# Local attention layers: scores from 64-row halves, the cosine product of q moved from VectorE to GpSimd, and the loop over four units written out

## The reference

```python
def l2norm(t):
    return t / jnp.maximum(jnp.linalg.norm(t, axis=-1, keepdims=True), 1e-12)
...
def attn_layer(x, Wqkv, qs, ksc, Wo):
    b, n, _ = x.shape
    qkv = x @ Wqkv
...
    q = l2norm(q) * qs
    k = l2norm(k) * ksc
...
    q = q * cos * scale + rotate_half(q) * sin * scale
    k = k * cos * inv + rotate_half(k) * sin * inv
    out = local_attention(q, k, v)
    out = out.transpose(0, 2, 1, 3).reshape(b, n, INNER)
    return out @ Wo
...
for i in range(DEPTH):
    x = attn_layer(shift_tokens(x), Wqkv[i], q_scale[i], k_scale[i], Wo[i]) + x
    x = ffn_layer(shift_tokens(x), ln_g[i], ln_b[i], W1[i], b1[i], W2[i], b2[i]) + x
```

## Time and profile before

| | |
|---|---|
| runs, device time | 4602.41 us median of 3 (4593.22 to 4614.95) |
| profiled execution | 4612.28 us, its span 4610.5 us |
| granted TensorE clock, mean | 0.955 |
| busy: PE / PEld / DVE / ACT / POOL | 4030.1 / 3106.3 / 3777.2 / 2589.8 / 2029.8 us |
| instructions | 117054 |
| DMA | 138.98 MB, 436100 packets; queue of instructions 3.44 + 1.06 MB |

### The profile page before, as it was taken

One profiled execution on the slowest core, in us unless ns is written; L12 is line 12 of the kernel. 1 busy time (PEld: TensorE's weight loads), 2 busy tenths in 40 slices (PEclk: granted clock), 3 DMA queues, 4 the chain that ended last, 5 costly groups with the idle time before them and its releaser, 6 DMA issues. The chain is left out here.

```text
span 4610.5 us, 117054 instructions
## 1 busy us (share of the span) xinstructions
PE 4030.1 (87%) x42352; PEld 3106.3 (67%) x42352; DVE 3777.2 (82%) x7533; ACT 2589.8 (56%) x4120; POOL 2029.8 (44%) x1420
## 2 busy tenths in 40 slices
PE   5998988989989989948858769989899899899898
PEld 4876867857858758615535558678588587586685
DVE  7988979979979979845325289899799799798897
ACT  4755746747747647512422457567477476475574
POOL 5644536635536446320010056355366354464452
PEclk9999999999999999977878989999999999999999
DMA  1111111111111101140030011111111111111111
GB/s 59 25 40 23 24 43 21 25 36 25 27 34 27 38 23 25 19 97 1 1 82 2 8 41 26 36 26 24 39 24 25 35 26 38 24 25 40 22 25 24
DMA packets 436100, 138.98 MB, mean 30 GB/s; under 512 B 413008, under 2 KB 419152, under 8 KB 433872
## 3 DMA queue, kind: packets, MB, share of 16 engines
q1 hardware_dynamic: 434608, 131.33, 13.2%
q10 hardware_dynamic: 1152, 3.15, 0.3%
HBM read 38.72 MB, written 1.05 MB: 9 GB/s over the span
## 5 line engine op out<-in xcount | busy, mean ns | idle before, releaser
L801 POOL TENSOR_TENSOR pool<-pool 128x512 f32<-128x512 f32 x768 | 1177.8, 1563 | 1158.7 <-DVE pool L900 1158.7
L470 PE MATMUL psum<-squares,pool 128*128 128x128 f32 x3072 | 703.0, 276 | 59.6 <-POOL pool L805 35.2
L472 PE MATMUL psum<-squares,pool 128*128 128x128 f32 x3072 | 694.9, 274 | 0.0
L715 ACT ACTIVATE pool<-psum 128x1024 f32<-128x1024 f32 x384 | 394.1, 1026 | 441.3 <-PE psum L515 441.3
L513 PE MATMUL psum<-wqkv_hi,xs_lo 128*128 128x512 f32 x1152 | 519.3, 451 | 114.1 <-DVE pool L900 44.8
L504 PE MATMUL psum<-pool 128*64 128x128 f32 x6144 | 539.8, 290 | 28.8 <-DMA pool<-pool 28.6
L676 ACT COPY pool<-psum 64x512 f32<-64x512 f32 x768 | 447.6, 583 | 206.3 <-PE psum L472 201.0
L889 DVE TENSOR_REDUCE pool<-pool 128x16 f32<-128x1024 f32 x384 | 451.5, 1211 | 102.1 <-ACT pool L715 101.4
L470 PEld LDWEIGHTS psum<-squares,pool 128*128 128x128 f32 x3072 | 430.8, 140 | 128.1 <-issue 48.9
L514 PE MATMUL psum<-wqkv_lo,xs_hi 128*128 128x512 f32 x1152 | 467.0, 405 | 0.0
L515 PE MATMUL psum<-wqkv_hi,xs_hi 128*128 128x512 f32 x1152 | 465.9, 404 | 0.0
(11 more groups left out here) (167 smaller groups left out, 7804.0 us busy)
## 6 DMA issues: line engine op xcount, KB each, us to landing
pool<-pool SPq DMA_DIRECT2D x768, 64.0 KB
pool<-pool SPq DMA_DIRECT2D x192, 128.0 KB, 2.4
pool<-in_wqkv SPq DMA_DIRECT2D x12, 1536.0 KB, 6.1
k_st<-turn_st SPq DMA_DIRECT2D x8, 1536.0 KB, 21.9
pool<-in_wo SPq DMA_DIRECT2D x12, 512.0 KB, 3.6
pool<-in_w SPq DMA_DIRECT2D x12, 341.0 KB, 3.0
pool<-in_w SPq DMA_DIRECT2D x12, 192.0 KB, 2.9
rotary<-in_rotary SPq DMA_DIRECT2D x2, 1024.0 KB, 5.3
```

The costliest lines, as they stand in the source:

```text
L470: pe.matmul(o, by_cos[:, p // 2, 2 * c:2 * c + 2, :], ident, start=True, stop=False, is_transpose=True)
L472: last = pe.matmul(o, by_sin[:, p // 2, 2 * c:2 * c + 2, :], ident, start=False, stop=True, is_transpose=True)
L801: last = g.tensor_tensor(by_sin[:, q, :, hd * r:hd * r + hd], qn[:, q, :, hd * (1 - r):hd * (2 - r)], tab, ALU.mult)
```

## The change

1. The cosine product of q goes from VectorE's step to GpSimd's. GpSimd now makes, for q and then for k, two sine halves and the cosine product; `cos_ready` counts twice a unit, and `k_cos_ready` is gone.
2. `kT` holds each pair of heads once. The score product of one head contracts over its own 64 rows and gives 64 columns, so there are two such products for each pair and window, in the two row halves of the array; even heads go to bank 4 and odd ones to bank 5. The copy of turned k is one of 128 rows (for two of 64), and GpSimd's copy of the last keys has half the elements. The probabilities' heads are in the new order (`at_h`). TensorE has a semaphore instruction of its own behind each wait for a copy of turned k.
3. The loop over four rounds is written out three times (a Python loop for `eng.Fori`), on every engine.

```diff
--- before.py
+++ after.py
@@ -126,7 +125,7 @@
 
         def plain(eng):
 
-            eng.sem_inc(passed_sp if eng is nc.sync else passed_pool, 1)
+            eng.sem_inc(passed_sp if eng is nc.sync else passed_pe if eng is nc.tensor else passed_pool, 1)
 
         def rsqrt(v, x, tmp, step, first, op0, c0, op1, c1, between=()):
 
@@ -278,7 +277,7 @@
             nwt = [cut(2 * HEADS) for _ in range(4)]
             qT = cut(PAIRS, P)
 
-            kT = [cut(PAIRS, 2, WIN + P) for _ in range(2)]
+            kT = [cut(PAIRS, WIN + P) for _ in range(2)]
             V = [cut(INNER) for _ in range(4)]
             v_last = [cut(INNER) for _ in range(2)]
             S = cut(HEADS, 2 * WIN)
@@ -315,8 +314,7 @@
 
             def tables(eng, layer):
 
-                eng.wait_ge(cos_ready, done(layer * UNITS - 1))
-                eng.wait_ge(k_cos_ready, done(layer * UNITS - 1))
+                eng.wait_ge(cos_ready, done(layer * UNITS - 1, 2, 1))
                 eng.wait_ge(sin_ready, done(layer * UNITS - 1, 2, 1))
                 eng.tensor_tensor(turn.rearrange("p t a e -> p t (a e)"),
                                   rotary[:].rearrange("p t a e -> p t (a e)"),
@@ -367,7 +365,7 @@
 
                 for k in range(3):
                     step(0, k, lambda d, k=k: k - d >= 0)
-                with eng.Fori(0, 3) as i:
+                for i in range(3):
                     for k in range(3, 7):
                         step(i, k, lambda d: True)
                 step(3, 3, lambda d: d >= 0)
@@ -424,9 +422,7 @@
                         sp.wait_ge(turn_ready, done(l + L0))
                         plain(sp)
                         sp.wait_ge(sin_ready, done(last, 2, 1))
-                        plain(sp)
-                        sp.wait_ge(cos_ready, done(last))
-                        sp.wait_ge(k_cos_ready, done(last))
+                        sp.wait_ge(cos_ready, done(last, 2, 1))
                         plain(sp)
                         load_projections(sp, l + 1)
                     layer(DEPTH - 1)
@@ -451,7 +447,7 @@
 
                             U = V0 + k
                             pe.wait_ge(sin_ready, done(U, 2, 0))
-                            pe.wait_ge(cos_ready, done(U))
+                            pe.wait_ge(cos_ready, done(U, 2, 0))
                             if isinstance(i, int) and i == 0 and k == 0:
                                 pe.wait_ge(x_ready, done(C0 - 1))
                             for p in range(4):
@@ -461,7 +457,7 @@
                                     if middle:
                                         middle()
                                     pe.wait_ge(sin_ready, done(U, 2, 1))
-                                    pe.wait_ge(k_cos_ready, done(U))
+                                    pe.wait_ge(cos_ready, done(U, 2, 1))
                                 if p >= 2:
                                     pe.wait_ge(t_out, done(U, 4, p - 2))
                                 for j in range(4):
@@ -484,11 +480,14 @@
                             for c in range(PAIRS):
                                 if c % 4 == 0:
                                     pe.wait_ge(t_out, done(U, 4, 2 + c // 4))
+                                    plain(pe)
                                 for w in range(NW):
-                                    o = bank(4 + c // 4)[WIN * w:WIN * w + WIN, P * (c % 4):P * (c % 4) + P]
-                                    last = pe.matmul(o, qT[:, c, WIN * w:WIN * w + WIN],
-                                                     kT[k % 2][:, c, :, WIN * w:WIN * w + 2 * WIN],
-                                                     start=False, stop=(c % 4 == 3))
+                                    for r in range(2):
+                                        rows = slice(64 * r, 64 * r + 64)
+                                        o = bank(4 + r)[WIN * w:WIN * w + WIN, 2 * WIN * c:2 * WIN * c + 2 * WIN]
+                                        last = pe.matmul(o, qT[rows, c, WIN * w:WIN * w + WIN],
+                                                         kT[k % 2][rows, c, WIN * w:WIN * w + 2 * WIN],
+                                                         start=False, stop=(c == PAIRS - 1))
                             last.then_inc(s_ready, 1)
 
                         def values(V0, i, k):
@@ -499,11 +498,11 @@
                             pe.wait_ge(y_ready, done(U - 1))
                             pe.wait_ge(kept[k % 2], kept_by(l + L0, i, k))
                             for h in range(HEADS):
-                                r = 64 * (h % 2)
+                                r, at_h = 64 * (h % 2), PAIRS * (h % 2) + h // 2
                                 o = bank(6 + h // 8)[r:r + 64, P * (h // 2 % 4):P * (h // 2 % 4) + P]
-                                pe.matmul(o, V[k % 4][:, DH * h:DH * h + DH], pT[:, h, :], start=True, stop=False)
+                                pe.matmul(o, V[k % 4][:, DH * h:DH * h + DH], pT[:, at_h, :], start=True, stop=False)
                                 last = pe.matmul(o[:, 0:WIN], v_last[k % 2][:, DH * h:DH * h + DH],
-                                                 pT_last[:, h, :], start=False, stop=True)
+                                                 pT_last[:, at_h, :], start=False, stop=True)
                             last.then_inc(o_ready, 1)
 
                         def step(i, k, has):
@@ -672,11 +671,8 @@
                                 if p == 2:
                                     a.wait_ge(k_kept, done(U))
                                 c = 4 * (p - 2)
-                                for r in range(2):
-                                    last = a.copy(kT[k % 2][64 * r:64 * r + 64, c:c + 4, r, WIN:WIN + P],
-                                                  bank(7 - p % 2)[64 * r:64 * r + 64, :]
-                                                  .rearrange("p (c t) -> p c t", c=4))
-                                last.then_inc(t_out, 1)
+                                a.copy(kT[k % 2][:, c:c + 4, WIN:WIN + P],
+                                       bank(7 - p % 2).rearrange("p (c t) -> p c t", c=4)).then_inc(t_out, 1)
 
                         def diagonal(U):
 
@@ -780,7 +776,7 @@
                             g.wait_ge(s_ready, done(U - 2))
                             b = kT[k % 2]
                             plain(g)
-                            g.tensor_copy(b[:, :, :, 0:WIN], b[:, :, :, P:P + WIN]).then_inc(k_kept, 1)
+                            g.tensor_copy(b[:, :, 0:WIN], b[:, :, P:P + WIN]).then_inc(k_kept, 1)
 
                         def step(i, k, has):
                             U = U0 + 4 * i + k
@@ -801,8 +797,8 @@
                                         last = g.tensor_tensor(by_sin[:, q, :, hd * r:hd * r + hd],
                                                                qn[:, q, :, hd * (1 - r):hd * (2 - r)], tab, ALU.mult)
                                     last.then_inc(sin_ready, 1)
-                                tab = turn[:, bass.ds(t, 1), 1, :].broadcast_to([P, HEADS, DH])
-                                g.tensor_tensor(by_cos[:, 1], qn[:, 1], tab, ALU.mult).then_inc(k_cos_ready, 1)
+                                    tab = turn[:, bass.ds(t, 1), q, :].broadcast_to([P, HEADS, DH])
+                                    g.tensor_tensor(by_cos[:, q], qn[:, q], tab, ALU.mult).then_inc(cos_ready, 1)
 
                         rest(U0, 0)
                         attention(g, step)
@@ -883,7 +879,6 @@
                             U = U0 + 4 * i + k
                             if has(0):
 
-                                t = 2 * i + k // 2
                                 for q in range(2):
                                     v.wait_ge(sq_ready, done(U, 2, q))
                                     last = v.tensor_reduce(ss[:, HEADS * q:HEADS * (q + 1)],
@@ -894,20 +889,13 @@
                                 rsqrt(v, ss, nwt, norm_step, done(U, RSQRT + 1, 0), ALU.max, 1e-24, None, None,
                                       between=probabilities(U - 2) if has(2) else ())
                                 v.wait_ge(sin_ready, done(U - 1, 2, 1))
-                                v.wait_ge(k_cos_ready, done(U - 1))
-                                v.wait_ge(cos_ready, done(U - 1))
+                                v.wait_ge(cos_ready, done(U - 1, 2, 1))
                                 for q in range(2):
                                     v.tensor_tensor(qn[:, q], bank(2 * q, 2).rearrange("p (h e) -> p h e", e=DH),
                                                     nwt[3][:, HEADS * q:HEADS * (q + 1)].unsqueeze(2)
                                                     .broadcast_to([P, HEADS, DH]), ALU.mult).then_inc(qn_ready, 1)
                                 if has(3):
                                     residual(U - 3, i, k - 3)
-                                if k == 0:
-                                    v.wait_ge(turn_ready, done(l + L0))
```

(4 more changed lines are left out.)

7 lines of the change are left out of this document (3 added, 4 removed).

## The result

The changed kernel takes **4645.01 us** (median of 6 runs, 4636.47 to 4651.14), the kernel before on the same chip 4606.92 (6 runs). The ratio is **1.0088, 95% interval 1.0069 to 1.0106**: 38 us slower. The profiled execution has a span of 4636.8 us, 26.3 more than the one before; its middle part, the global attention, which the change does not touch, happens to be 14 us shorter (from the scaling of the sixth layer's last round, L894, to the first of the seventh layer 778.5 us, before 792.4). Outside of it the changed kernel is thus 40 us slower.

A forecast was written before the change was run, and what follows sets the result against it. VectorE and TensorE were taken as full, VectorE and GpSimd excluding each other at the port. Per layer 13 x 0.33 + 1.5 + 0.65 - 0.6 = 5.8 us, twelve +70; 4612.3 gives 4682, less 10 to the median: 4672 us, range 4590 to 4740.

The forecast's parts named there:

- The port: VectorE instructions with two SBUF inputs or plain scalar ones and any GpSimd instruction exclude each other; removed 2.43 us returns as waits.
- It gets the gap at 7.69 and is done at 7.8: Steady round: first Newton step (L149 before), asked for at 7.61, runs between GpSimd's sine halves of k, a gap 0.08 wide.
- 16.05 or 16.25 a round: Steady round between scalings of q and k: 16.05 us, 0.33 above 15.72; 16.25 as bound if L149 misses the gap.
- The alternation that the prediction chose: Steady round: from L158 on, GpSimd's copy L775 gets in between VectorE's instructions; if VectorE kept the port, 15.65 us.
- "Nothing" for part 2 in steady rounds: Single copy of turned k saves ScalarE 1.2 us a unit and TensorE's 0.39 wait, but ends no VectorE wait: no gain.
- TensorE "15.2 each ... about 0.8 of room": TensorE busy 15.2 us per steady round, so about 0.8 of room in a round of 16.05.
- the rival: TensorE decides: port does not bind, or L157's wait falls under 0.85 us; round 14.7, about 4445 us; chance 0.10.
- Scores "2.0, no change": Scores in 64-row halves stay at 2.0 us a unit on TensorE; bounds 1.0 and 4.0.
- the dearest rival: Each score record keeps its cost: scores 4.0 us, TensorE's round 17.2, 230 us more, about 4830 us; chance 0.05.
- Loop written out at 0: Writing out the loop over rounds changes nothing; fetching the longer program costed at 0, up to 1 us a layer.
- First rounds +2.15: First two rounds of each layer: +1.5 us in the first (to 14.45), +0.65 in the second (15.41 to 16.05).
- Tail -0.6: Layer's end: copies of turned k save 0.6 us in the chain to the last L876, where VectorE waits 0.61.

The follow-up runs named there:

- e1: Kernel before with only q's cosine product moved to GpSimd; scores, copies and loop as before: 4662.93 us, ratio 1.0103.
- e9: Changed kernel's scores, copies and written-out loop, with q's cosine product on VectorE between the scalings of q and k: 4508.9 us, ratio 0.979.
- e10: Changed kernel with GpSimd's cosine product of k made for one head of sixteen, a probe that omits part of the rotation: 4398.77 us, ratio 0.9556.
- e2: Changed kernel with the move undone, q's cosine product back on VectorE behind the residual; 64-row scores, single copy, written-out loop stay: 4554.44 us, ratio 0.9868.
- e5: Changed kernel with the two softmax sums put ahead of the first two Newton steps: 4610.76 us, ratio 1.0011.
- e8: Kernel before with 64-row scores and single kT, loop written out on TensorE alone: 4567.32 us, ratio 0.9913.
- e12: Kernel before with q's cosine product between the two scalings on VectorE and softmax sums first; old scores, copies, hardware loop: 4566.91 us, ratio 0.9914.
- e3: Kernel before with only 64-row scores and single kT, hardware loop kept: 4675.43 us, ratio 1.0139.
- e4: Kernel before with only the loop over four rounds written out: 4602.92 us, ratio 0.9976.
- e7: Changed kernel with the mean product of chunk 0 at each layer's end made three times instead of once: 4631.33 us, ratio 1.0045.

## Why the prediction was right, and where its terms were off

The sign holds, the total is near (forecast 4672, measured 4645, 1.5% and 0.9% slower), and the mechanism, products that wait for each other at the port, is the one that the runs show. The terms are another matter. The forecast's 70 us were 51 in steady rounds, 26 in first rounds and -7 in tails; measured are 5, 18 and 16. The term that carried the forecast is almost gone, since part 2 gave back what the move cost, and the tails, which were to gain, lost. That the sum is near is in good part luck.

- **The port** was right, and is shown from three sides: the product alone costs (e1), its place alone gives (e9), and a shorter GpSimd product makes two 32-column instructions of VectorE short again (e10). Priced against the same kernel without the move (e2), the steady round pays 0.35 us. That the prediction said 0.33 is chance: it meant the kernel before, against which it is 0.03, and its 16.05 would be 0.63 above e2.
- **"It gets the gap at 7.69 and is done at 7.8"** failed. L148 was asked for at about 7.9 after the scaling, and the gap was at 7.6. That is the case the prediction kept as a bound, at 16.25 (its 12.3 and 3.85 make 16.15; from L157 to the next scaling have 3.95). The wait sits on L148 and L149, not on L156, which is L157 of before (0.21).
- **16.05 or 16.25 a round**: 15.76. GpSimd's last product ends 11.25 after the scaling, not 11.55, since no gap is lost to L149 and L150; and the two small copies, 0.7 us in the sum, run beside the reduction L830, which needs no port. From the first L840 to the next scaling it is 3.54 us, as forecast (3.55). The alternation that the prediction chose without a row for it shows in e5, where the copies do meet VectorE's run (L771 0.60, L156 0.40).
- **"Nothing" for part 2 in steady rounds** was the wrong term of most weight. Through the shorter L783 it gives 0.2 to 0.3 us a round (e2 against before 0.32, of which the loop has 0.08; e8 against before 0.22). This was hidden in the forecast, as its round was built from GpSimd's end with the short copy already in it, and compared with before.
- **TensorE "15.2 each ... about 0.8 of room"** left out the 0.39 that lies in TensorE's own circle. Its round was 15.63 (e12). In the forecast this decided nothing; in the rival it did: with the wait gone TensorE's bound is 14.75, and e10, whose round of 14.71 is at that bound, shows the rival's world at 4399 us, where 4445 was given. Its condition, a wait under 0.85 us, was worked out with the 15.2; no run tests it.
- **Scores "2.0, no change"**: a block of 128 products takes 1.61 us for the 1.96 of 64 (L492 in e3 and L489 in e12, above). The upper bound of 4.0, and with it the dearest rival, is excluded; the lower of 1.0 is as well. The Trainium skill's factor of 2 (TensorEngine Tiling (Array Packing), Theoretical Speedup) is 1.2 here for a block of twice the products and half their columns.
- **Loop written out at 0** is nearly right for the loop alone (e4, 0.08 us a round) and leaves out what it does for part 2, which loses 1.4% without it (e3).
- **First rounds +2.15**: +1.53. The first alone was given +1.5 and pays 0.7; the place of the wait is right, 2.27 us on L149 behind the cosine product (timeline of VectorE, first layer, below).

```profile
57.96 0.87 DVE L148 TENSOR_SCALAR pool<-pool 128x32 f32<-128x32 f32 x1
...
58.87 2.27 DVE L149 TENSOR_SCALAR pool<-pool 128x32 int32<-128x32 int32 x1
...
63.49 2.36 DVE L894 TENSOR_TENSOR pool<-psum,pool 128x1024 f32<-128x1024 f32 x2
```

- **Tail -0.6**: +1.6. The last maximum waits 0.22 us for the scores, for 0.61 in the earlier trace rows, but starts only 0.1 us earlier behind the scaling (18.3 for 18.4) where the clock stays up. At nine tails of twelve TensorE runs values at the lower clock, 1.55 us each, which no term of the prediction had. The rest, some 0.7 us a tail, lies behind the maximum.

## What to carry to other kernels

Where VectorE and GpSimd share the port, busy time does not tell who works: look for tiny instructions that take a microsecond, and lay both timelines over each other. Moving a product to the idle engine gains nothing when the wait comes back later; gain comes from order, with port-free work (reductions, reads of PSUM) on VectorE where GpSimd runs, and products where it has not begun. Before a unit that is relieved is expected to pay, price the second limit with its own waits in it, and check that a loop's body still fits when the number of instructions grows.

## What the runs showed of the hardware that was not expected

- An unrelated-looking edit of 64 more products a round made each turn of TensorE's hardware loop cost 2.8 to 6.1 us (e3), and nothing before, at some 1640 instructions a body against 2158. Part of it is the lower clock that followed each stand-still of 3.6 to 4.5 us.
- A GpSimd copy shortened by 0.22 us (L783, 0.41 for 0.63) shortened the VectorE instruction behind it by 0.23 us (L149, 0.38 in e2 for 0.61 in e4), means over all steady rounds.
- In the changed kernel TensorE's granted clock went to 1.2 GHz after idle stretches of 0.71 and 2.15 us with 1.1 us of products between, and the values products behind them started every 0.64 us for 0.35. Three times the product in between (e7) kept the clock up in that place at all twelve tails, and the last maxima came 1.55 us earlier at the nine that had been low.
